# Main attention of a two-layer network: the probabilities turned by VectorE in 32x32 squares, the values' product in 32-row tiles

## The reference, cut to what matters

```python
q = (rmsnorm(hidden @ q_a_w.T, q_a_ln_w) @ q_b_w.T)      # 16 heads, 128 + 64 rotary
kv_a = hidden @ kv_a_w.T                                  # 64 latent + 16 x 64 rotary keys
kv = rmsnorm(kv_a[..., :64], kv_a_ln_w) @ kv_b_w.T        # keys and values from 64 latents
scores = jnp.einsum('bhqd,bhkd->bhqk', qf, kf) * scale    # qf, kf with the rotary parts
probs = softmax(scores, axis=-1)
ctx = jnp.einsum('bhqk,bhkd->bhqd', probs, v)
main_out = ctx.transpose(...).reshape(b, s, H * D_V) @ o_w.T
```

## Time and profile before

| | us |
|---|---|
| median of 3 runs | 1297.78 (1294.37 to 1297.87) |
| the profiled execution | 1291.33 |
| its span in the trace | 1289.5 |
| PE busy | 1243.0 (96%) |
| VectorE busy | 768.3 (60%) |
| ScalarE busy | 732.9 (57%) |
| GpSimd busy | 533.4 (41%) |

### The profile page before, as it was taken

One profiled execution on the slowest core, in us unless ns is written; L12 is line 12 of the kernel. 1 busy time (PEld: TensorE's weight loads), 2 busy tenths in 40 slices (PEclk: granted clock), 3 DMA queues, 4 the chain that ended last, 5 costly groups with the idle time before them and its releaser, 6 DMA issues.

```text
span 1289.5 us, 22502 instructions
## 1 busy us (share of the span) xinstructions
PE 1243.0 (96%) x8298; PEld 875.0 (68%) x8298; DVE 768.3 (60%) x1254; ACT 732.9 (57%) x1370; POOL 533.4 (41%) x531
## 2 busy tenths in 40 slices
PE   8999999999999999999999998999998998999997
PEld 5544334477777777777777777889753444678997
DVE  4689978245454444445454666555667763855555
ACT  3479978855555555555555635332355676435553
POOL 5266274248576666767666124443100000512211
PEclk9999999999999999999999999999999999989999
DMA  7780000001101011111111021020233310101111
GB/s 287 200 180 2 2 19 11 10 18 29 38 22 38 22 38 27 32 32 32 29 36 54 25 72 76 27 72 12 74 74 88 72 38 1 34 17 33 50 42 34
DMA packets 40887, 64.44 MB, mean 50 GB/s; under 512 B 8221, under 2 KB 27421, under 8 KB 39837
## 3 DMA queue, kind: packets, MB, share of 16 engines
q1 hardware_dynamic: 40776, 62.99, 17.8%
HBM read 45.60 MB, written 8.45 MB: 42 GB/s over the span
## 4 chain that ended last, share of the span: by engine, by line
PE 85%; DVE 8%; ACT 3%; issue 2%; DMA 1%; POOL 1%; SPq 0%; ACTq 0%; DVEq 0%; POOLq 0%
PE bank L1951 9%; PE bank L1883 9%; PE bank L1513 8%; PE bank L2151 6%; PE bank L2152 6%; PE bank L2153 6%; PE bank L1604 5%; PE bank L1850 5%; PE bank L1852 5%; PE bank L1851 5%; PE bank L1470 4%; PE bank L1333 3%; PE bank L1974 2%; PE bank L1450 2%; DVE mpc L1412 2%
## 5 line engine op out<-in xcount | busy, mean ns | idle before, releaser
L1859 DVE TENSOR_REDUCE nmq<-bank 128x1 f32<-128x1024 f32 x128 | 155.8, 1217 | 151.8 <-PE bank L1852 151.8
L1491 ACT ACTIVATE Pb<-bank 128x512 f32<-128x512 f32 (+3 forms) x355 | 180.6, 573 | 30.2 <-PE bank L1470 9.3
L1896 ACT ACTIVATE Pt<-bank 128x512 f32<-128x512 f32 x187 | 110.7, 594 | 118.8 <-PE bank L1883 117.9
L1874 ACT ACTIVATE Pq<-bank,nmq 128x1024 f32<-128x1024 f32 x127 | 141.7, 1116 | 58.7 <-DVE nmq L1859 58.7
L1341 DVE TENSOR_REDUCE mp<-bank 128x2 f32<-128x1024 f32 x128 | 153.5, 1221 | 27.5 <-PE bank L1333 26.7
L1883 PE MATMUL bank<-idf,Pq 128*128 128x128 f32 x1016 | 145.7, 275 | 1.4 <-ACT Pq7l L1874 1.2
L1883 PEld LDWEIGHTS bank<-idf,Pq 128*128 128x128 f32 x1016 | 119.1, 140 | 36.5 <-issue 11.9
L1412 DVE TENSOR_REDUCE mpc<-bank 128x2 f32<-128x1024 f32 (+2 forms) x96 | 88.4, 953 | 46.3 <-PE bank L1400 23.2
L1951 PE MATMUL bank<-Pt,kvx 128*64 128x256 f32 x992 | 114.1, 382 | 0.0
L1850 PE MATMUL bank<-qk1h,qk0h 128*128 128x512 f32 x256 | 109.4, 427 | 0.4 <-ACT Pq L1874 0.4
L1513 PE MATMUL bank<-Pb,vx 128*17 128x256 f32 (+3 forms) x1222 | 106.3, 407 | 0.7 <-ACT OTa L1527 0.5
(11 more groups left out here) (374 smaller groups left out, 2951.7 us busy)
## 6 DMA issues: line engine op xcount, KB each, us to landing
t<-t SPq DMA_DIRECT2D x128, 64.0 KB, 2.0
wr<-wf SPq DMA_DIRECT2D x25, 256.0 KB, 2.6
wraw<-wf SPq DMA_DIRECT2D x8, 768.0 KB, 4.6
scratch<-stgr SPq DMA_DIRECT2D x4, 1024.0 KB, 4.0
Rs<-shares SPq DMA_DIRECT2D x64, 64.0 KB, 2.7
scratch<-stg SPq DMA_DIRECT2D x8, 384.0 KB, 2.6
qst<-scratch SPq DMA_DIRECT2D x9, 256.0 KB, 8.4
owT<-owT SPq DMA_DIRECT2D x1, 2048.0 KB, 11.2
```

The costliest lines, as they stand in the source:

```text
L1491: e.activation(PBR[l][i % len(PBR[l])][:, 0:c], bank[b][:, 0:c], ACT.Exp, scale=0.25).then_inc(exp_ok[0], 1)
L1859: e.tensor_reduce(nmq[:, n % 8:n % 8 + 1], scores(u, i), AX, ALU.max, negate=True).then_inc(mp_ok, 1)
L1874: e.activation(probabilities(u, i)[:], scores(u, i), ACT.Exp, bias=nmq[:, n % 8:n % 8 + 1], accum_out=sums[:, u % 2, i:i + 1]).then_inc(ex ...
```

## The change

PE turns nothing any more in this stage. Instead VectorE turns each tile of probabilities (128 queries x 1024 keys) in 32x32 squares with one instruction, SBUF to SBUF (L1838): `PT[u % 2][:, b, c:c + 32]` then holds, for key block b of 32 keys, in partitions 32g to 32g + 31 those keys against the 32 queries of row group g. The values' product runs over 32 key blocks, 4 row groups g and 2 heads: 256 matmuls of 32 rows, 64 weight columns and 64 moving columns a unit (L1905), each row group into its own PSUM bank (4 to 7), each head into its half of the partitions. The 64 latents are needed in all four row groups: 16 DMAs make the four `kv4` copies once, at the beginning of the stage. `ot` reads all four banks; the projection takes bank 7 and the preparations banks 5 and 6, so that each waits for what stood there. There are three buffers of probabilities in place of eight, two of turned ones of 128x4096 in place of ten of 128x512. The copies are gone from ScalarE.

The order is written anew. In unit u: score 0, preparation, [rec and turn 3 of unit u - 1], exponential 0, score 1, preparation, spread, turn 0, exponential 1, score 2, `pv` of u - 1, turn 1, `ot`, exponential 2, score 3, `project` and `add` of u - 1, exponential 3, preparation, turn 2. Not every place for a preparation is taken: `PREP_AT` gives the quarters of units.

```diff
-PREP_EVERY = 5
-BY_VECTOR = (0, 6)
+PREP_AT = ((4, 5, 7, 9, 11, 13), (-1, 1, 4, 7, 9, 12))
...
+    preps = {16 * (p - 1) + at: (p, i) for p in range(1, 8) for i, at in enumerate(PREP_AT[p > 1])}
...
+    for u in range(1, 32):
+        order.append(("score", u, 0))
+        prep(4 * u)
+        order.extend([("rec", u - 1), ("vturn", u - 1, 3), ("expo", u, 0)])
+        order.extend(BESIDE_LAST.get((u, 0), ()))
+        order.append(("score", u, 1))
+        prep(4 * u + 1)
+        order.extend([("spread", u - 1), ("vturn", u, 0), ("expo", u, 1)])
+        order.extend(BESIDE_LAST.get((u, 1), ()))
+        order.extend([("score", u, 2), ("pv", u - 1), ("vturn", u, 1), ("ot", u - 1), ("expo", u, 2)])
+        order.extend([("score", u, 3), ("project", u - 1), ("add", u - 1), ("expo", u, 3)])
+        prep(4 * u + 3)
+        order.append(("vturn", u, 2))
...
     def act_expo(e, u, i):
         n = 4 * u + i
         e.wait_ge(mp_ok, n + 1)
-        if n >= 8:
-            e.wait_ge(tr_mm, 8 * (u - 2) + 8)
+        if n >= 3:
+            e.wait_ge(pt_ok, n - 2)
...
+    def dve_turn(e, u, i):
+
+        c, n = 64 * (i % 2) + 32 * (i // 2), 4 * u + i
+        e.wait_ge(exp_ok[1], n + 1)
...
+        source = probabilities(u, i)[:].rearrange("p (b k) -> p b k", k=32)
+        if u < 31:
+            e.transpose(PT[u % 2][:, :, c:c + 32], source).then_inc(pt_ok, 1)
+        else:
+            e.transpose(PTl[0][:, :, c:c + 32], source[:, 0:16, :])
+            e.transpose(PTl[1][:, :, c:c + 32], source[:, 16:32, :]).then_inc(pt_ok, 1)
...
+    def sp_values(e):
...
+        for s in range(4):
+            for g in range(4):
+                e.dma_start(kv4[s][32 * g:32 * g + 32, :, :], kvx[32 * s:32 * s + 32, :, :]).then_inc(d_kv, 16)
...
-        e.wait_ge(pta_ok, (u + 1) * (NT - len(BY_VECTOR)))
-        e.wait_ge(ptv_ok, (u + 1) * len(BY_VECTOR))
-        for k in range(NT):
-            for hd in range(2):
-                last = e.matmul(bank[6][64 * hd:64 * hd + 64, 0:256], kvx[:, k, :],
-                                transposed(u, k)[:, 256 * hd:256 * hd + 256],
-                                start=(k < 1), stop=(k == NT - 1), skip_group_check=True)
+        e.wait_ge(*COPIED[u])
+        e.wait_ge(pt_ok, 4 * u + 4)
+        for b in range(32):
+            for g in range(4):
+                rows = slice(32 * g, 32 * g + 32)
+                for hd in range(2):
+                    cs = slice(64 * hd, 64 * hd + 64)
+                    last = e.matmul(rest[cs, g, 0:64], kv4[b % 4][rows, b // 4, :], transposed(u, b)[rows, cs],
+                                    start=(b == 0), stop=(b == 31), skip_group_check=True)
         last.then_inc(pv_mm[1], 1)
```

More of the change, by code:

```diff
@@ L74 @@
 BESIDE_LAST = {
[L75 to L80, removed]
+    (29, 0): [("temperature",), ("wup", 0), ("wdown", 0)],
+    (31, 0): [("stats", 0)],
+    (31, 1): [("normed", 0)],
 }
+PREP_AT = ((4, 5, 7, 9, 11, 13), (-1, 1, 4, 7, 9, 12))
 def main_order():
-    order = [("expo", 0, 1), ("score", 0, 2), ("score", 0, 3), ("ctx", 0), ("ctx", 1), ("expo", 0, 2), ("cadd", 0),
-             ("ctx", 2), ("expo", 0, 3), ("cadd", 1), ("ctx", 3), ("cadd", 2), ("cadd", 3)]
@@ L92, in main_order @@
[L92 to L136, removed]
@@ L137, in main_order, with prep @@
-    assert not chunks
-    order.extend([("pv", 31)] + BESIDE_LAST[31, "values"] + [("ot", 31)])
-    output(31)
+    order = [("expo", 0, 1), ("score", 0, 2), ("ctx", 0), ("ctx", 1), ("vturn", 0, 0), ("expo", 0, 2), ("score", 0, 3),
+             ("cadd", 0), ("ctx", 2), ("vturn", 0, 1), ("cadd", 1), ("expo", 0, 3), ("ctx", 3), ("cadd", 2), ("vturn", 0, 2),
+             ("cadd", 3)]
+    preps = {16 * (p - 1) + at: (p, i) for p in range(1, 8) for i, at in enumerate(PREP_AT[p > 1])}
+    def prep(n):
+        if n in preps:
+            order.extend([("prep", *preps[n]), ("pcopy", *preps[n])])
@@ L140, in main_order @@
+    order.extend([("turn", 0), ("rec", 31), ("vturn", 31, 3), ("spread", 31), ("pv", 31), ("hT", 0), ("wup", 1), ("wdown", 1),
+                  ("ot", 31), ("project", 31), ("logits", 0), ("add", 31)])
     return order
@@ L365, in program @@
     wide = [nc.alloc_psum_tensor(f"bank{2 * i}", [128, 2, 512], F32) for i in range(2)]
-    bank = [wide[i // 2][:, i % 2, :] for i in range(4)] + [nc.alloc_psum_tensor(f"bank{i}", [128, 512], F32)[:] for i in range(4, 8)]
+    rest = nc.alloc_psum_tensor("bank4", [128, 4, 512], F32)
+    bank = [wide[i // 2][:, i % 2, :] for i in range(4)] + [rest[:, i, :] for i in range(4)]
     x = sb("x", [128, NT, D], F32)
@@ L493, in program @@
     hn1 = sb("hn1", [128, 4, D], F32, at=WSP)
[L495 to L505, removed]
+    P = [MP.sb("P0", [128, T], F32)] + [sb(f"P{i}", [128, T], F32, at=S0 + (76 + 4 * i) * 1024) for i in (1, 2)]
+    PT = [sb("PT0", [128, 32, 128], F32, at=S0 + 64 * 1024), sb("PT1", [128, 32, 128], F32, at=HTP)]
+    PTl = [sb(f"PTl{i}", [128, 16, 128], F32, at=at) for i, at in enumerate((KV, WKPE))]
+    kv4 = [sb(f"kv4{i}", [128, NT, 64], F32, at=at) for i, at in enumerate((W0A, HN, MP.at, S0 + 88 * 1024))]
     OTm = sb("OTm", [128, 256], F32, at=LNW)
@@ L1616, in pe_prep @@
     def pe_prep(e, p, k):
-        b, free = PTB["prep", p, k]
+        b, free = PREP[p, k]
         e.wait_ge(*free)
+        e.wait_ge(pc_ok, len(FIRST) * p + k - 1)
         pe_part(e, p, FIRST[k], bank[b][:], (0, 1))
@@ L1973, in pe_project_out @@
         for q in range(2):
-            last = e.matmul(bank[b][:, 256 * q:256 * q + 256], OTm[:, 128 * q:128 * q + 128], mo[:, u // 4, :],
+            last = e.matmul(bank[7][:, 256 * q:256 * q + 256], OTm[:, 128 * q:128 * q + 128], mo[:, u // 4, :],
                             start=True, stop=True)
@@ L2826, in vector @@
                 dve_score(e, s[1], s[2])
[L2827 to L2828 removed]
+            elif s[0] == "vturn":
+                dve_turn(e, s[1], s[2])
             elif s[0] == "rec":
```

94 lines of the change are left out of this document (32 added, 62 removed).

## The result

| | before | after |
|---|---|---|
| median of 4 runs each | 1296.07 us (1292.83 to 1297.87) | 1571.43 us (1565.34 to 1575.49) |
| profiled span | 1289.5 us | 1573.7 us |
| step of one unit | 15.17 us | 23.98 us |
| granted clock in 384 to 720 us | 1.00 | 0.78 |

A forecast was written before the change was run, and what follows sets the result against it. PE's queue was taken to bound the kernel. Units at 14.0 us with late shares, 12.3 without, gave 426 against 470.4 us; gain 44, beginning 3, end loss 2: 1246 us profiled, 1252 us median, range 1210 to 1320.

The forecast's parts named there:

- The failed step: Values' product on PE: 512 passes in eight tiles side by side, 3.9 us a unit against 3.60 before.
- The array's term: PE's time for the values' product: 64 passes a tile at 0.058 us, eight tiles at once, 3.7 us.
- rival 2: PE's instruction supply in the values' product: four packets at 1.2 us, 4.9 us; +15, 1267 us; chance 0.14.
- The worse case: PE's instruction packets requested only when their place is free: some 6.3 us for the product, +45, 1297 us.
- My unit without late shares: One unit of the stage with no swap near it on SP's queue: 12.3 us.
- the loop as I drew it: Maximum, exponential, third score, product, fourth score, its maximum, addition, turn, next unit's first maximum: 12.3 us, product wholly inside.
- PE's own queue: PE's work in a unit: scores, product of 3.9, projection and preparations, 12.0 us.
- The shares: Softmax shares over HBM, delayed by swaps on SP's queue: units of 15.3, 14.1, 14.1 and 12.3 us, 14.0 each.
- the turn: VectorE's large turn of 128x1024 f32 probabilities: 1.23 us, ends of the range 0.7 and 1.8 us.
- rival 4: Values' product with only four of eight tiles at once: 7.4 us, +75, 1327 us; chance 0.16.
- rival 5: Values' product passes enter one by one at 0.058 us, 25.8 us more a unit, about 2050 us; chance 0.05.
- VectorE's load: VectorE's work in a unit: maxima, large turns, reciprocal, weighting and addition, 10.7 us.

The follow-up runs named there:

- experiment 2: Kernel of its own with only long runs of small PE products: 1,536 float32 passes in eight tiles took 42.5 us, 768 bfloat16 passes 19.1 us.
- The quarter: The changed kernel with the values' product over only the first 8 of 32 key blocks: 1307.4 us.
- the half: The changed kernel with the values' product over only the first 16 of 32 key blocks: 1336.3 us.
- experiment 4: The changed kernel with the product over 8 of 32 key blocks, each unit's sums weighted by the shares of the unit before: 1237.1 us.
- the wide form: The changed kernel with 128 product matmuls of 32 rows by 128 weight columns in place of 256, half the result unusable: 1336.9 us.

## Why the prediction was wrong

**The failed step is the values' product:** "with 0.15-0.2 for the change of form 3.9 us". It takes 13.6 us: the step had a term for the array and none for the supply of its instructions. The array's term was too small: 58 ns a pass in one tile was right, but eight tiles side by side take 11 ns where 7.3 was taken, so 5.6 us at full clock in place of 3.7. Measured are 7.9 us of work, at a lowered clock in part, and 5.6 us without instructions. These are not causes side by side. A block comes every 3.5 to 3.75 us whatever its passes cost below 28 ns, with 8 ns a pass in bfloat16 (experiment 2) as with 11 or 16 ns here. So at the 7.3 ns that I took the product would have been nearly as long, which is an inference: the supply is what failed.

**It was rival 2, at three times its price.** I had the mechanism, its sign (gaps at each 256th instruction) and the right count of packets, four. I priced a packet by its own time, 1.2 us, four in 4.9 us. The worse case, as long again to arrive, I put at 6.3 us, which is 2.4 us once on top of 3.9; by its own condition it is four times 2.4 us, 9.8 us, 5.9 more a unit and some 180 us in all, so slower. The period is 3.5 to 3.75 us. The records show the next packet starting only about a microsecond after the block before began to run (up to 1.7 in the long runs), then 0.9 to 1.5 us of transfer and 1.3 to 1.6 us until PE goes on. The earlier trace rows gave only how long packets take; how soon one follows another could have been read, in the packet records, only where PE was hungry, and before it never was. My point against it, that PE had no idle time and so no packet came late, was true and said nothing: the earlier trace rows has 2,165 matmuls and 2,164 loads in 336 us, 13 instructions a microsecond, the new product asks for 1,024 in 3.9 us, 263 a microsecond, and 256 in 3.6 us are 71. The Trainium skill (Runtime: NRT & Kernel Launch, "Instruction fetch mechanics") has both readings, 128 KiB for PE and "only 2 cache lines"; the runs agree with the second: 267 passes, 534 instructions, is the most that ran at 11 ns a pass without a stop, far from 2,048. It also says that fetching is hidden since instructions are issued more slowly than they arrive; here 256 leave in 1.5 us and the next 256 take 3.5, so the measurement decides against it.

**The clock.** I had said that a fall would spoil every term. It was 0.78 in the stage, 0.58 in the later blocks of a product. Behind the product six score passes take 0.43 us in place of 0.23 and the projection 1.55 in place of 0.87, 1.9 us a unit.

**The sum, again.** My unit without late shares was 12.3 us with a product of 3.9. With 13.6 it is 12.3 + 9.7 = 22.0, with the slower passes behind it 23.9; measured 23.98. That agreement doesn't show the loop as I drew it. PE's own queue, which I had at 12.0 us, gives 12.0 + 9.7 + 1.9 = 23.6 in the same way, and PE is what has no room left (331.2 of 336 us). The chain goes through VectorE and ScalarE in some units (718.9 to 723.2 us), with the projection in place of the fourth maximum; in others (626.9 to 651.0 us) it never leaves PE. The product stands whole in either path, so that each microsecond of it was one of the unit; that part was right.

**The shares** were hidden behind the product, so their term dropped out. The quarter shows that the path exists and that I made it 1.8 us a unit too short. With a product as I had forecast, the kernel would have come out near the quarter's 1307 us or the half's 1336, not at 1252: an inference, since neither run has a whole product. So a second step was wrong, and by this estimate (31 x 1.8 = 56 us against a gain of 45) alone it would have taken the gain away.

**Right:** the turn (1223 ns forecast as 1.23 us), the tiles side by side (rivals 4 and 5 fell: 11 ns a pass, where rival 4 had 14.5 and rival 5 had 58), and VectorE's load of 10.7 us a unit (276.7 / 336 x 13.28 = 10.9 in experiment 4). The 25 ns between starts of the Trainium skill (TensorE: Matmul & The Clock Gate, "Wait — 56ns, not 53.3ns?") don't hold between different tiles, as the earlier trace rows had said. By it the product would have been 12.8 us, near the 13.6 measured; that is a coincidence, since within a block passes start every 11 ns.

**A version that beats both** did not come out. The best with the whole product's columns, the wide form, is bound by the array at 16.76 us a unit against 15.17. Two units' queries behind one weight load would halve the instructions at the same array work, but by my count four buffers of turned probabilities don't fit beside the rest; it was not tried.

## What to carry to other kernels

Count instructions as well as array time. On PE, 256 instructions (128 f32 passes in this form) cost some 3.5 us at least once a stretch is longer than about 500 of them, so passes shorter than about 28 ns each buy nothing there; a weight load and matmul pair should last that long, or the stretch be short. When a change makes many small instructions out of few large ones, write down instructions per microsecond for the new stretch beside the largest such rate in the trace of before, and treat a rate that no row shows as a cost, not as free. And before trusting a gain, work out the next path in the same detail as the one removed: here both were under-priced.
